# Two half-attentions joined into one run of 32 turns, with split x kept in DRAM and the root as a power

## The reference

```python
x = x + tanh(g_xattn[0]) * attention(layernorm(x), ctx, mask, Wq, Wk, Wv, Wo)
# attention, per batch: 16 heads of 128, 8 k/v heads (two heads share one)
q, k, v = layernorm(x) @ Wq, ctx @ Wk, ctx @ Wv
out = softmax(where(mask, q k^T / sqrt(128), -inf)) @ v
return out @ Wo
```

## Time and profile before

| | us |
|---|---|
| median of 3 runs | 4127.5 |
| lowest and highest | 4120.8, 4129.4 |
| profiled execution | 4139.6 |
| its span | 4137.1 |
| PE busy in the span | 3677.3 (89%) |
| VectorE, ScalarE, GpSimd busy | 2389.9, 1845.7, 1469.5 |
| first half, its 16 turns and start | 0 to 753 |
| second half | 753 to 1520 |

### The profile page before, as it was taken

One profiled execution on the slowest core, in us unless ns is written; L12 is line 12 of the kernel. 1 busy time (PEld: TensorE's weight loads), 2 busy tenths in 40 slices (PEclk: granted clock), 3 DMA queues, 4 the chain that ended last, 5 costly groups with the idle time before them and its releaser, 6 DMA issues. The chain is left out here.

```text
span 4137.1 us, 70813 instructions
## 1 busy us (share of the span) xinstructions
PE 3677.3 (89%) x23412; PEld 3159.1 (76%) x23412; DVE 2389.9 (58%) x6409; ACT 1845.7 (45%) x4748; POOL 1469.5 (36%) x1554
## 2 busy tenths in 40 slices
PE   7999999699999978059999995799999959999999
PEld 6999999688998868059999994566666647777777
DVE  6666666566666656046666665788888633222221
ACT  4444444344444431035555552577777732222222
POOL 3333333233333322335665664455555520000000
PEclk9999999899999985579999997899999969999999
DMA  2111110211111125056666664111111020000000
GB/s 90 54 36 35 53 35 28 100 37 36 36 54 36 36 71 120 0 182 230 230 220 239 220 227 178 46 49 65 52 48 65 17 105 31 21 21 21 20 21 21
DMA packets 146147, 329.67 MB, mean 80 GB/s; under 512 B 18337, under 2 KB 31522, under 8 KB 145474
## 3 DMA queue, kind: packets, MB, share of 16 engines
q1 hardware_dynamic: 107586, 240.56, 17.0%
q10 hardware_dynamic: 23488, 45.16, 3.3%
q0 software_dynamic: 14912, 42.12, 2.7%
HBM read 263.92 MB, written 63.88 MB: 79 GB/s over the span
## 5 line engine op out<-in xcount | busy, mean ns | idle before, releaser
L444 POOL TENSOR_SCALAR a_prob<-a_prob,a_rinv 128x256 f32<-128x256 f32 x512 | 467.7, 926 | 941.6 <-DVE a_rinv L516 941.6
L407 ACT ACTIVATE a_prob<-a_prob,a_nbias 128x256 f32<-128x256 f32 x512 | 256.7, 502 | 562.0 <-DVE a_nbias L509 562.0
L1097 DVE TENSOR_TENSOR e_w_lo<-e_w_raw,e_w_hi 128x1024 fp32r<-128x1024 f32 (+1 forms) x316 | 333.2, 1095 | 59.2 <-ACT e_w_hi L1055 59.0
L1003 PE MATMUL e_gb<-e_xt_hi,e_w_hi 128*128 128x256 f32 x1248 | 357.1, 286 | 10.6 <-DVE e_xt_lo L1097 10.2
L2057 DVE TENSOR_TENSOR f_h_lo<-f_h_f,f_h_hi 128x512 fp32r<-128x512 f32 x128 | 92.1, 720 | 459.7 <-ACT f_h_hi L2033 459.7
L1004 PE MATMUL e_gb<-e_xt_lo,e_w_hi 128*128 128x256 f32 x1248 | 354.9, 284 | 0.0
L1005 PE MATMUL e_gb<-e_xt_hi,e_w_lo 128*128 128x256 f32 x1248 | 354.8, 284 | 0.0
L278 PE MATMUL a_pj<-a_xt_hi,a_wq_hi 128*128 128x256 f32 x1024 | 309.6, 302 | 0.3 <-DVE a_q_lo L452 0.2
L2031 ACT ACTIVATE f_h_f<-f_hb,f_b_sb 128x512 f32<-128x512 f32 x128 | 88.2, 689 | 487.1 <-PE f_hb L1956 427.2
L279 PE MATMUL a_pj<-a_xt_lo,a_wq_hi 128*128 128x256 f32 x1024 | 287.3, 281 | 0.0
L280 PE MATMUL a_pj<-a_xt_hi,a_wq_lo 128*128 128x256 f32 x1024 | 286.7, 280 | 0.0
(11 more groups left out here) (360 smaller groups left out, 11593.3 us busy)
## 6 DMA issues: line engine op xcount, KB each, us to landing
e_w_raw<-in_w_gate SPq DMA_DIRECT2D x40, 2048.0 KB, 11.8
e_w_raw<-in_w_out SPq DMA_DIRECT2D x40, 1024.0 KB, 5.5
a_x_sb<-in_x SPq DMA_DIRECT2D x32, 512.0 KB, 6.3
d_y_sb<-y_rows SPq DMA_DIRECT2D x16, 1024.0 KB, 5.2
a_ctx_raw<-in_ctx_t SPq DMA_DIRECT2D x32, 256.0 KB, 6.4
a_xr_sb<-in_x SPq DMA_DIRECT2D x16, 512.0 KB, 5.1
x_half<-a_xo_sb ACTq DMA_DIRECT2D x16, 512.0 KB, 5.7
a_xr_sb<-x_half SPq DMA_DIRECT2D x16, 512.0 KB, 4.7
```

Source lines behind the costliest of these rows:

```text
L407: e = nc.scalar.activation(prob[:, u % 4, t], prob[:, u % 4, t], ACT.Exp, bias=nbias[:, u % 2, t:t + 1], scale=SCALE, accum_out=rsum[:, u ...
L444: p = nc.gpsimd.tensor_scalar(prob[:, u % 4, t], prob[:, u % 4, t], rinv[:, u % 2, t:t + 1], None, ALU.mult)
L1003: nc.tensor.matmul(out, a_hi, b_hi, start=start, stop=False)
L1097: return nc.vector.tensor_tensor(out, raw, hi.bitcast(F32), ALU.subtract)
```

## The change

Both halves become one run of 32 turns (turn n works on batch n mod 16; from turn 16 on with heads 8 to 15). A step is still one head, now from -9 to 260; `all_steps` writes out the start, loops over 7 pairs, writes out pair 7 (steps 117 to 132), loops over 7 pairs, and writes out the last.

Weights are 10 pieces a half of 1024 columns each, loaded into their own tile `w_raw` (three rooms); for the first half's start four more rooms are `xo_sb` and `xr_sb`. Pieces 0 to 5 get their low part on VectorE, all others on GpSimd. The second half's pieces 10 to 19 are split in the steps that `SPLIT` names, 118 to 132; ScalarE waits first for the last PE use of what it overwrites, PE waits for each piece at its first new use, and SP waits for a free room before each further load.

In turns 0 to 15 the split, transposed x (both parts in one tile `xt`, 1 MB) is stored to DRAM by SP; in turns 16 to 31 it is loaded from there, and statistics, root, xn and x's transposes and copies are not done (`ONLY`). The root is one GpSimd operation, (var + eps) to the power -0.5; VectorE adds eps at -9, GpSimd follows in that step, xn stays at -7. The mask's conversion moves from -9 to -2. Loads of the start are reordered: x, ctx, four pieces, mask, three pieces, x and ctx of turn 1, the rest; the gate is loaded from ScalarE's queue.

The core of the diff (4 blanks of indentation less):

```diff
+def gated_cross_attention(nc, x_in, x_half, x_out, xt_rows, ctx_t, mask, gate, wq, wk, wv, wo, identity, tag):
 HEADS = NHEAD0 // 2
 GROUPS = HEADS // 2
-C0 = half * HEADS * DH0
-G0 = half * GROUPS * DH0
+TURNS = 2 * B
...
+    w_raw = sb("w_raw", [P, 3, 1024])
...
+    var, rstd, power = sb("var", [P, 2]), sb("rstd", [P, 2]), sb("power", [P, 2])
...
-    xt_hi, xt_lo = sb("xt_hi", [P, 2, FC, S], F32R), sb("xt_lo", [P, 2, FC, S], F32R)
+    xt = sb("xt", [P, 2, 2, FC, S], F32R)
...
-    pieces = [(wk[:, :, G0:G0 + GROUPS * DH0], wk_hi[:], wk_lo[:]), (wv[:, :, G0:G0 + GROUPS * DH0], wv_hi[:], wv_lo[:])]
-    for c in range(0, FC, 2):
-        pieces.append((wq[:, c:c + 2, C0:C0 + HEADS * DH0], wq_hi[:, c:c + 2], wq_lo[:, c:c + 2]))
-    for h in range(0, HEADS, 4):
-        pieces.append((wo[:, half * HEADS + h:half * HEADS + h + 4], wo_hi[:, h:h + 4], wo_lo[:, h:h + 4]))
...
+    def pieces_of(half):
+        k0, q0, h0 = half * KW, half * QW, half * HEADS
+        found = [(wk[:, :, k0:k0 + KW], wk_hi[:], wk_lo[:]), (wv[:, :, k0:k0 + KW], wv_hi[:], wv_lo[:])]
+        for h in range(0, HEADS, 2):
+            cols = slice(h * DH0, (h + 2) * DH0)
+            found.append((wq[:, :, q0 + h * DH0:q0 + (h + 2) * DH0], wq_hi[:, :, cols], wq_lo[:, :, cols]))
+        for h in range(0, HEADS, 2):
+            found.append((wo[:, h0 + h:h0 + h + 2], wo_hi[:, h:h + 2], wo_lo[:, h:h + 2]))
+        return found
+    pieces = pieces_of(0) + pieces_of(1)
+    WK, WV, WQ, WO, SET = 0, 1, 2, 6, 10
+    ON_DVE = 6
+    ROOMS = ["r0", "r1", "r2", "xo0", "xo1", "xr0", "xr1", "r0", "r1", "r2"] + [f"r{n % 3}" for n in range(SET)]
+    SPLIT = {-9: (0,), -8: (1,), -7: (2,), -5: (3,), -4: (4,), -3: (5,), -2: (6,), -1: (7,), 1: (8,), 2: (9,),
+             118: (10,), 120: (11,), 121: (12,), 123: (13,), 125: (14,), 127: (15,), 128: (16,), 129: (17,), 131: (18,), 132: (19,)}
...
+    WHEN = {"load_x": -11, "load_ctx": -11, "load_res": -2, "load_xt": -9, "keep_xt": -4, "stats": -9, "mask": -2, "xn": -7, "ctx": -8,
+            "x0": -6, "x1": -5, "k0": -4, "k1": -3, "v0": -2, "v1": -1, "out": 12}
+    SHARED = ("x0", "x1", "k0", "k1", "v0", "v1")
+    ONLY = {"load_x": (2, B), "load_ctx": (2, TURNS), "load_res": (1, TURNS), "load_xt": (B, TURNS), "keep_xt": (0, B),
+            "stats": (0, B), "xn": (0, B), "x0": (0, B), "x1": (0, B)}
+    FIRST, AHEAD = -9, 5
+    LAST = TURNS * HEADS + 5
...
     def all_steps(eng, step):
+        half = B // 2
         for u in range(FIRST, AHEAD):
-            step(0, u, False)
-        with eng.Fori(0, B // 2 - 1) as i:
-            for u in range(AHEAD, PAIR + AHEAD):
-                step(i, u, False)
-        for u in range(AHEAD, PAIR + AHEAD):
-            step(B // 2 - 1, u, True)
+            step((0, 0, 0), u)
+        with eng.Fori(0, half - 1) as i:
+            for u in range(AHEAD, AHEAD + PAIR):
+                step((i, 0, half - 2), u)
+        for u in range(AHEAD, AHEAD + PAIR):
+            step((half - 1, half - 1, half - 1), u)
+        with eng.Fori(half, 2 * half - 1) as i:
+            for u in range(AHEAD, AHEAD + PAIR):
+                step((i, half, 2 * half - 2), u)
+        for u in range(AHEAD, LAST - PAIR * (2 * half - 1)):
+            step((2 * half - 1, 2 * half - 1, 2 * half - 1), u)
...
+        low_done(sp, 5)
+        load_residual(start, 0)
+        low_done(sp, 6)
...
+            for bb in due(f, u, "load_xt"):
+                sp.wait_ge(pj_ready, made(f, bb - 2, HEADS - 1))
                 sp.nop(nofuse=True)
-                load_residual(b, bb)
+                sp.wait_ge(xt_kept[bb % 2], 16 * (B // 2))
+                b = bass.ds(at(f, lambda k: 2 * k + bb - B), 1)
+                sp.dma_start(xt[:, bb % 2].bitcast(F32), xt_rows[b].rearrange("o p h c s -> p (o h) c s")).then_inc(xt_loaded[bb % 2], 16)
+            for bb in due(f, u, "keep_xt"):
+                sp.wait_ge(pj_lod, made(f, bb, "x1"))
+                sp.nop(nofuse=True)
+                b = bass.ds(turn(f, bb, 0), 1)
+                sp.dma_start(xt_rows[b].rearrange("o p h c s -> p (o h) c s"), xt[:, bb % 2].bitcast(F32)).then_inc(xt_kept[bb % 2], 16)
+            for bb in due(f, u, "load_res"):
+                sp.wait_ge(o_free, turn(f, bb, 1))
+                sp.nop(nofuse=True)
+                if same(f, lambda k: (2 * k + bb) // B):
+                    sp.wait_ge(x_stored[bb % 2], at(f, lambda k: 16 * ((2 * k + bb - B) // 2) + 32))
+                    sp.nop(nofuse=True)
+                load_residual(f, bb)
+            if f[1] == f[2] and PAIR * f[1] + u == 117:
+                for n in range(SET, SET + 3):
+                    load(n)
+            for n in splits(f, u):
+                if SET + 3 <= n + 3 < 2 * SET:
+                    load(n + 3)
...
+            if fresh(f, bb) and h % 2 == 0:
+                low_done(pe, set_of(f, bb) + WQ + h // 2)
...
+            if fresh(f, bb) and h % 2 == 0:
+                low_done(pe, set_of(f, bb) + WO + h // 2)
...
+            if n == SET + WK:
+                act.wait_ge(pj_ready, number[B - 1, "k1"] + 1)
+            elif n == SET + WV:
+                act.wait_ge(pj_ready, number[B - 1, "v1"] + 1)
+            elif SET + WQ <= n < SET + WO:
+                act.wait_ge(pj_ready, number[B - 1, 2 * (n - SET - WQ) + 1] + 1)
+            elif n == 2 * SET - 1:
+                act.wait_ge(o_ready, B)
+            elif n >= SET + WO:
+                act.wait_ge(w_used, n - SET - WO + 1)
+            act.wait_ge(w_loaded[n % 7], 16 * (n // 7 + 1))
+            nc.scalar.copy(pieces[n][1], raw(n)).then_inc(w_hid, 1)
+        def high(f, bb, use):
+            act.wait_ge(pj_ready, made(f, bb, use))
+            if use in ("x0", "x1") and not (f[1] == f[2] and 2 * f[1] + bb < 2):
+                act.wait_ge(xt_kept[bb % 2], at(f, lambda k: 16 * ((2 * k + bb) // 2)))
+            nc.scalar.copy(item(bb, use)[0], item_psum(f, bb, use)).then_inc(pj_hid, 1)
...
+            for bb in due(f, u, "stats"):
+                pool.wait_ge(stat_link, at(f, lambda k: 3 * (2 * k + bb) + 3))
+                pool.nop(nofuse=True)
+                nc.gpsimd.tensor_tensor(rstd[:], var[:], power[:], ALU.pow).then_inc(root_done, 1)
+            for n in splits(f, u):
+                if n >= ON_DVE:
+                    pool.wait_ge(w_hid, n + 1)
+                    nc.gpsimd.tensor_tensor(pieces[n][2], raw(n), pieces[n][1].bitcast(F32), ALU.subtract).then_inc(w_lod_pool, 1)
...
-                inverse_root(dve, nc.vector, chain, at + 3, mv[:, :, 1], LN_EPS, root, rstd[:], n - 1)
...
+                dve.wait_ge(stat_link, at(f, lambda k: 3 * (2 * k + bb) + 2))
+                nc.vector.tensor_scalar(var[:], mv[:, :, 1], LN_EPS, None, ALU.add).then_inc(stat_link, 1)
...
+            for bb in due(f, u, "mask"):
+                mask_of(f, bb)
+            for bb in due(f, u, "xn"):
+                dve.wait_ge(root_done, turn(f, bb, 1))
+                for t in range(2):
+                    l = nc.vector.tensor_scalar(xn[:, t], x_sb[:, bb % 2, t], mv[:, t, 0:1], rstd[:, t:t + 1], ALU.subtract, ALU.mult)
+                l.then_inc(xn_done, 1)
...
-for half, (x_res, x_out) in enumerate(((a["x"], x_half), (x_half, x1))):
-    gated_cross_attention(nc, half, a["x"], x_res, x_out, a["ctx_t"], a["mask"], a["g_xattn0"], by_row(a["wq0"]), by_row(a["wk0"]), by_row(a["wv0"]),
-                          by_row(a["wo0"]), a["identity"], f"a{half}_")
+gated_cross_attention(nc, a["x"], x_half, x1, dram("xt_rows", [B, P, 2, D // P, S]), a["ctx_t"], a["mask"], a["g_xattn0"], by_row(a["wq0"]),
+                      by_row(a["wk0"]), by_row(a["wv0"]), by_row(a["wo0"]), a["identity"], "a_")
```

More of the change, by code:

```diff
@@ L171, in gated_cross_attention @@
-        for j in range(SHARED):
-            plan(j - SHARED, "shared", j)
-        FIRST, AHEAD = min(WHEN), 5
-        def due(u, last, what):
-            batches = range(2) if u < AHEAD or last else range(4)
-            return [(bb, n) for bb in batches for w, n in WHEN.get(u - HEADS * bb, []) if w == what]
-        def here(u, last):
-            return 0 <= u < PAIR or (u >= PAIR and not last)
+        def pieces_of(half):
[7 more added lines that the diff above has]
+            return found
@@ new lines, in raw_free, with low_done, at @@
+        def raw_free(eng, n):
+            was = [k for k in range(n) if ROOMS[k] == ROOMS[n]]
+            if was:
+                low_done(eng, was[-1])
+        def low_done(eng, n):
+            if n < ON_DVE:
+                eng.wait_ge(w_lod, n + 1)
+            else:
+                eng.wait_ge(w_lod_pool, n - ON_DVE + 1)
+        def at(f, of):
+            reg, lo, hi = f
+            v = of(lo)
+            step = of(hi) - of(hi - 1) if hi > lo else 0
+            assert all(of(k) == v + step * (k - lo) for k in range(lo, hi + 1))
+            return reg * step + (v - step * lo) if step else v
@@ new lines, in gated_cross_attention, with live, due, head @@
```

(30 more changed lines are left out.)

433 lines of the change are left out of this document (206 added, 227 removed).

## The result

The changed kernel takes 4029.97 us (median of 4 runs, 4023.8 to 4032.37); the kernel before, on the same chip, 4125.51. The ratio is 0.9767, with a 95% interval of 0.975 to 0.9784. The forecast was 4031, from a base of 4127.5. The profiled execution took 4030.16 (span 4028.1), 109 less than the profiled one of before, 4139.6. The attention accounts for 95.3 of that: its last residual add stands at 1424.57, before at 1519.87. The other 13.7 lie behind it, in code that the change leaves alone.

A forecast was written before the change was run, and what follows sets the result against it. PE was taken to bound both attention halves and to wait between them. Savings of 27.9 + 14.9 + 44.7 + 9.3 = 96.8 us from a median of 4127.5 gave 4031, own range 4020 to 4045, overall range 4014 to 4060.

The forecast's parts named there:

- Part A: Second half: x kept split in DRAM removes layer norm, transposes and their copies from turns 16 to 31; 27.9 us.
- I keep 5.6: Second half: VectorE's "issue" gaps, which look like instruction loading, stay at 5.6 us, between 0 and 16.
- 4 x 6.05 + 4 x 4.66 = 42.84: Turn without x: four k/v projection steps and four plain ones, 42.84 us, 2.15 less than 44.99.
- Part B: First half: root as a GpSimd power takes back PE's whole stall in x steps; 14.9 us, between 0 and 17.
- two steps of 4.66 + 0.5: First half: the two steps that turn x lose their stall, giving a turn of 43.84 us.
- Part C: Seam between the halves: 176.2 us become three turns without x plus 3 us of swapping; 44.7 us, 27 to 48.
- That is 0.2 a step; I take 0.5: Seam: ScalarE's piece copies lengthen six plain steps, 0.5 us each taken, so 3 us, between 0 and 20.
- one of my signs that C is wrong: Seam: bias operations of over 1 us standing in steps 118 to 132 would show the seam's forecast wrong.
- Part D: Start: earlier PE start, some 4 us, and a shorter second gap, 5; 9 us, between 2 and 14.
- The swap isn't hidden: Seam rival: each of 10 POOL subtractions locks a bias out for 2.3 us, 23 instead of 3; 4051; chance 0.13.
- The stall kept: First half and start, rival: VectorE stays late and waits for POOL; some 2 us instead of 24; 4053; chance 0.15.
- More gained: Second loop and seam, rival: instruction idle goes and the seam costs nothing, 8.6 us more; 4022; chance 0.11.
- Slower by the power: POOL's power, rival: a slow one locks biases out 16 times; slower from 8.4 us, 4154 at 10; chance 0.03.

The follow-up runs named there:

- experiment 1: Changed kernel with one unused tile of 32 bytes a partition ahead of ctx_raw, moving ctx and the tiles behind it: 4003.81 us, ratio 0.9739.
- experiment 12: Changed kernel with the root again as 12 VectorE operations, ctx_raw and all behind it placed as the 32-byte pad put them: 4021.94 us.
- 3: Changed kernel without the split x in DRAM; turns 16 to 31 load, normalize, transpose and split x again, with the power: 4034.14 us, ratio 0.9809.
- 8: Changed kernel with the mask's conversion back at step -9 behind the statistics, loads in their new order: 4023.74 us.
- 9: Kernel before with 48 empty VectorE instructions ahead of each half's step list: 4122.66 us.
- 2: Changed kernel with the root again as 12 VectorE operations, ctx and all behind it moved by 128 bytes: 4026.58 us, ratio 0.9794.
- experiment 4: Changed kernel with each of the second half's ten weight pieces copied twice on ScalarE and subtracted twice on GpSimd: 4040.47 us, ratio 0.9819.
- experiment 5: Changed kernel with the power computed four times in a row on GpSimd: 4013.93 us.

## Why the prediction was right, and where its parts were not

The median came within 1.1 us of the forecast, and the attention's marks within 1.5 (95.3 for 96.8). The sum is better than its terms, and that is luck: A and C gave 0.8 and 1.9 us more than forecast, B and the last two turns 3.5 and 0.8 less, and the largest two errors cancel inside A.

A turn of the second half took 45.42 us before. It is made up by the runs like this: 42.82 of PE's work at good places (experiments 1 and 12), 0.90 for turning x (3), 1.01 for the root chain (12), 0.43 of the gaps, and 0.25 that is left. That last is 44.99 - 44.74, before's first half against experiment 12. Most of it stands in PE's recorded waits for `a_ot_lo`: 26 of 8.1 us in before's 13 turns, 20 of 5.2 in experiment 12's. What else makes VectorE late there is not found; the mask operation alone, with the power, was worth 0.05 (8). The changed kernel pays 42.82 plus 0.39 for its places.

- *PE-bound, and the marks to read it by*: right. No wait of PE is left between 80 and 1400 us. The turns were to read 43.8 and 42.8 and read 44.1 and 43.2.
- *Part A*, 27.9 forecast and 28.7 measured, holds two errors that cancel. "I keep 5.6" was wrong: the gaps went, 5.6 gained, and I had no row that said why they should. "Instruction loading" fits what the trace has beside the gaps (9). "4 x 6.05 + 4 x 4.66 = 42.84" was wrong for these places by 0.37 a turn, 4.8 lost. The 42.84 was right for the layout that its rows come from, where a plain step takes 4.64; experiment 1 has the same 4.64 and 42.82. The load of the split x at nothing is right (3). What A's edit is worth depends on B. With the chain still there it takes 1.9 a turn (44.74 - 42.82, experiment 12), and with the power there only 0.90 (3): the rest is the stall, which the power takes away as well. I counted it once, in the order A then B, but a reader of "part A: 27.9" would think it all the split x's.
- *Part B*, 14.9 forecast and 11.4 measured. Gap and refill went as forecast: the "two steps of 4.66 + 0.5" measure 5.13 and 5.14 for 5.16. The miss lies in the other six steps of the turn, 6.08 to 6.13 for 6.05 and 4.70 for 4.66, by the places of the tiles; 13 x 0.27 = 3.5 us is all of it. At experiment 1's places the period is 43.73 and B 16.3.
- *Part C*, 44.7 forecast and 46.6 measured. "That is 0.2 a step; I take 0.5" was too dear: the copies and subtractions cost nothing net, since 3 x 43.21 = 129.6 is the whole seam. The overlap of bias and subtraction, put at "nearly nil", is 0.43 and 0.85 us in two of ten pieces. So one of my signs that C is wrong, a bias of over 1 us in the seam, did appear (1.02 us at 745.14), and C isn't wrong: the sign was badly chosen, since PE's step around it keeps its 4.70.
- *Part D*, 9.3 (written 9) forecast and 9.4 measured. The first gap gave the 4.0 that I took, though the "12.7" behind it would be 4.6 and PE started at 13.26. The rest of the start gave 5.4 for 5, of which 4.2 is the second gap. The root has some 2 of the whole (2, 12). The mask I had named among the things ahead of the first xn and not priced: left at its old step under the new order of loads it would have cost 5.0 (8).
- *The swap isn't hidden* (4051): didn't happen, but is near. It decides at about twice the work a piece; experiment 4 has it, with 12 us. The Trainium skill (SBUF — State Buffer, "Who interferes with whom") has the lock held for a whole instruction, and 700.24 + 2.42 against the bias's end at 702.68 agrees. The trace of experiment 5 doesn't: there the bias ran inside a power of 0.69 us, and the measurement decides.
- *The stall kept* (4053): no; two xn in a row and a wait for GpSimd don't make VectorE late, as the loop of 4.41 us had said.
- *More gained* (4022): both its gains came (8.6 us; that a shorter loop is the reason of the first was not shown), and the places took them back. Experiment 1 is that case, 11.5 us better than after.
- *Slower by the power*: its price is 0.7 to 1.0 us, and four in a row cost nothing. The break-even of 8.4 us rested on a lock that a power of 0.69 us did not take.

## What to carry to other kernels

Where PE is the bound, price a helper's work by how long it makes PE stand, and give a stall to one edit only: two edits that each remove the same lateness are worth less together than the sum of what each is worth alone. A turn's length read at one layout of SBUF is good to about 1% at another; when a turn is longer and nobody waits, move the tiles by 32 bytes before looking for a cause in the work. Weights can be swapped piece by piece under running turns if a copy and a subtraction of each fit once into a step, and not twice.

## What the hardware showed that I had not expected

- The same matmuls run up to 0.9% faster or slower by the place of the operands in SBUF: a turn of 43.21 us became 42.82, 42.95, 43.21 and 43.15 with tiles moved by 32, 64, 96 and 128 bytes, with no wait recorded; 0, 32 and 128 bytes repeat within 0.01.
- GpSimd's power of 2 columns takes 0.69 to 0.98 us, and a VectorE bias of 0.17 us ran its normal time while such a power ran (472.52 inside 472.30 to 472.99, and in 14 turns more). The same bias took 2.13 us under a subtraction of 2.41, and a mask operation of 0.29 us took 2.27.
- A store and a load of 1 MB, landing in 4.8 and 4.9 us, beside a PE-bound turn cost nothing that its period shows (44.11 with and without).
- VectorE's gaps of up to 3.1 us in the kernel before stay when its instructions are moved by 48. Each holds the start of an 8 KB instruction packet that falls beside a load of data; the changed kernel's loops have neither packets nor gaps.
